# Decoder layer on one core: the first sequence's cross-attention maxima are split one tile sooner, and their transfer is issued ahead of the next queries' pieces

## The reference

```
x = x + self_attention(layernorm(x))          # 16 heads of 16, 4 key/value heads, causal, rotary
x = x + cross_attention(layernorm(x), ctx)    # 16 heads of 16, keys and values from ctx, int mask
x = x + ffn(layernorm(x))                     # relu(x w1 + b1), rounded to a 4-3 float, times rounded w2

q, k = rope(q), rope(k)                       # products with cosines and sines, and their sum
scores = q k^T * 16**-0.5, masked             # -inf above the diagonal, or -1e9 where mask == 0
out = softmax(scores) v, then an output projection and a bias
```

## Time and profile before

| | |
|---|---|
| median of three runs | 1729.31 us |
| profiled execution | 1726.77 us, of which the span from first to last instruction 1725.1 us |
| PE busy | 1617.5 us, 94% |
| PEld / DVE / ACT / POOL busy | 56% / 67% / 65% / 44% |
| granted clock of TensorE, mean | 0.982 of full speed |
| SP's DMA queue | 130.96 MB, 51.0% of 16 engines' span |
| chain that ended last | PE 75%, DMA 9% (of the span, Q<-negT 5%), ACT 6%, DVE 4% |

### The profile page before, as it was taken

How to read it: one execution, slowest core, us unless ns; L and a number is a source line. 1 busy time by engine, 2 the same in 40 slices (tenths; PEclk the granted TensorE clock), 3 DMA queues, 4 the chain that set the end, 5 groups by cost and what they waited for, 6 DMA issues and landing times.

```text
span 1725.1 us, 33722 instructions
## 1 busy us (share of the span) xinstructions
PE 1617.5 (94%) x11950; PEld 973.6 (56%) x11950; DVE 1159.0 (67%) x1736; ACT 1116.1 (65%) x1733; POOL 753.5 (44%) x1010
## 2 busy tenths in 40 slices
PE   3879999999999999999999999999999999999988
PEld 2445556656555565655656555665655556565555
DVE  4557576685857758586676858668585775857573
ACT  4455675766668566665856567576666856666574
POOL 2252344644345553444545334464434555344410
PEclk7979999999999999999999999999999999999999
DMA  7473453754547374553845546375454737454420
GB/s 182 59 99 70 68 85 65 103 95 64 96 60 107 68 96 90 75 84 57 119 72 81 94 66 89 65 103 95 64 96 60 106 68 96 90 75 73 62 40 13
DMA packets 106238, 140.17 MB, mean 81 GB/s; under 512 B 12385, under 2 KB 74242, under 8 KB 105954
## 3 DMA queue, kind: packets, MB, share of 16 engines
q1 hardware_dynamic: 103090, 130.96, 51.0%
q0 software_dynamic: 2352, 8.26, 1.5%
q10 hardware_dynamic: 768, 0.57, 0.1%
HBM read 21.29 MB, written 8.39 MB: 17 GB/s over the span
## 4 chain that ended last, share of the span: by engine, by line
PE 75%; DMA 9%; ACT 6%; DVE 4%; issue 3%; POOL 2%; SPq 1%; DVEq 0%; ACTq 0%; POOLq 0%
PE o_pair L1457 14%; PE score L1418 8%; PE small L1543 7%; DMA Q<-negT 5%; PE small L1577 5%; PE o_pair L1288 5%; PE small L1288 4%; PE score L1395 3%; PE small L1304 3%; PE score L1341 3%; DVE negmax L1021 2%; PE score L1376 2%; PE small L1470 2%; DMA sums<-o_sb 2%; PE score L1400 2%
## 5 line engine op out<-in xcount | busy, mean ns | idle before, releaser
L1021 DVE TENSOR_REDUCE negmax<-score 128x4 f32<-128x1024 f32 (+1 forms) x384 | 456.9, 1216 | 73.4 <-PE score L1376 47.0
L780 ACT ACTIVATE P<-score 128x1024 f32<-128x1024 f32 x448 | 446.4, 1026 | 74.6 <-PE score L1418 26.4
L1053 DVE TENSOR_TENSOR P<-P,cross_bound 128x1024 f32<-128x1024 f32 x192 | 230.8, 1250 | 88.6 <-ACT P L780 88.5
L1457 PE MATMUL o_pair<-P,V 128*32 128x256 f32 (+1 forms) x4096 | 280.0, 362 | 2.6 <-DVE P L1053 2.4
L828 ACT ACTIVATE score<-cross_q 128x1024 f32<-128x1024 bf16 x192 | 196.3, 1023 | 46.4 <-DVE negmax L1021 42.9
L1418 PE MATMUL score<-Q,K 99*128 99x256 bf16 x1024 | 152.3, 276 | 25.9 <-DMA Q<-negT 24.8
L1457 PEld LDWEIGHTS o_pair<-P,V 128*32 128x32 f32 x4096 | 87.8, 108 | 134.6 <-issue 73.4
L1577 PE MATMUL small<-xnT,w 128*128 128x256 f32 x600 | 157.6, 381 | 0.0
L1418 PEld LDWEIGHTS score<-Q,K 99*128 99x128 bf16 x1024 | 83.7, 98 | 125.7 <-ACT P L780 61.7
L558 POOL TENSOR_TENSOR x<-x,ffn 128x1024 f32<-128x1024 f32 x15 | 32.8, 2189 | 268.9 <-DVE negmax L1021 268.9
L1376 PE MATMUL score<-K,Q 96*128 96x256 bf16 x768 | 121.0, 282 | 9.9 <-ACT score L828 5.4
(11 more groups left out here) (202 smaller groups left out, 3049.4 us busy)
## 6 DMA issues: line engine op xcount, KB each, us to landing
K<-k2p SPq DMA_DIRECT2D x96, 256.0 KB, 6.2
Q<-q2p SPq DMA_DIRECT2D x192, 128.0 KB, 5.2
Q<-q1p SPq DMA_DIRECT2D x90, 256.0 KB, 6.7
x_in<-in_x SPq DMA_DIRECT2D x16, 512.0 KB, 5.3
ctxT<-in_ctx SPq DMA_DIRECT2D x16, 512.0 KB, 7.1
k2f<-q1f SPq DMA_DIRECT2D x32, 256.0 KB, 6.3
inT<-o_sb SPq DMA_DIRECT2D x60, 128.0 KB
o<-inverse SPq DMA_DIRECT2D x60, 128.0 KB
```

The costliest lines, as they stand in the source:

```text
L780: A.activation(P[:, t % 4, :], score[b][:, :, :], ACT.Exp, scale=SCALE).then_inc(score_free[b], 1)
L1021: V.tensor_reduce(negmax[:, k, h:h + 1024 // w], s.rearrange("p (h w) -> p h w", w=w), AX.X, ALU.max, negate=True).then_inc(score_free[b], 1)
L1053: V.tensor_tensor(p, p, cross_bound[:, t % 2, :].unsqueeze(1).broadcast_to([128, 4, SEQ]), ALU.min).then_inc(probs_masked[1], 1)
L1457: last = T.matmul(o_ps[ob][32 * j:32 * j + 32, SEQ * gg + q0:SEQ * gg + SEQ], v, p, start=s == 0, stop=end, tile_position=(0, 32 * j), ski ...
```

## The change

Three orders are changed; no instruction is added or taken away.

- On ACT, in the plain cross scores: `cut_first` of the first sequence stands ahead of tile 10's premask instead of behind it, `cut_second` behind that premask instead of behind tile 11's premask and eviction, and `maxima` behind tile 12's premask and eviction instead of behind tile 13's premask.
- On POOL: `cut_rest` stands between the products and the sum of the rotated keys, and `cut_third` behind that sum. Before, both stood behind the first query piece.
- On SP: `put_neg` of the first sequence stands ahead of the three transfers of the first query piece instead of behind them.

```diff
--- before.py
+++ after.py
@@ -458,9 +458,9 @@
                 if nxt:
                     sp.wait_ge(small_full[st.bank("v2_1")], st.this("v2_1"))
                     sp.dma_start(ctxT[:, :, :], ctx_v[i + 1]).then_inc(ctx_loaded, 16)
+                put_neg(st, 1, 0)
+                if nxt:
                     put_part("q1", 0, i + 1)
-                put_neg(st, 1, 0)
-                if nxt:
                     put_part("k1", 0, i + 1)
                     put_part("q1", 1, i + 1)
                     put_part("k1", 1, i + 1)
@@ -644,11 +644,12 @@
                     rope_products("q1", cosq, sinq, q1s, i + 1)
                     rope_sum("q1", q1s, i + 1)
                     rope_products("k1", cosk, sink, k1s, i + 1)
+                cut_rest(1, i, 0)
+                if nxt:
                     rope_sum("k1", k1s, i + 1)
+                cut_third(1, i, 0)
+                if nxt:
                     part("q1", 0, whole, part1, i + 1)
-                cut_rest(1, i, 0)
-                cut_third(1, i, 0)
-                if nxt:
                     rest("q1", i + 1)
                     part("k1", 0, whole, part1, i + 1)
                     part("q1", 1, rest1, part2, i + 1)
@@ -934,15 +935,15 @@
                 if prev:
                     hidden(st, [2])
                 for t in range(3, N2):
+                    if t == 10:
+                        cut_first(1, i, 0)
                     if t not in PE_MASKED:
                         premask(i, t)
                     if prev and t in EVICT_AFTER:
                         hidden(st, [3 + EVICT_AFTER.index(t)])
                     if t == 10:
-                        cut_first(1, i, 0)
-                    if t == 11:
                         cut_second(1, i, 0)
-                    if t == 13:
+                    if t == 12:
                         maxima(st, 1, 0)
                 if prev:
                     ffn_out(st, 0)
```

More of the change, by code:

```diff
@@ L460, in body @@
                     sp.dma_start(ctxT[:, :, :], ctx_v[i + 1]).then_inc(ctx_loaded, 16)
-                    put_part("q1", 0, i + 1)
                 put_neg(st, 1, 0)
                 if nxt:
+                    put_part("q1", 0, i + 1)
                     put_part("k1", 0, i + 1)
@@ L646, in body @@
                     rope_products("k1", cosk, sink, k1s, i + 1)
+                cut_rest(1, i, 0)
+                if nxt:
                     rope_sum("k1", k1s, i + 1)
-                    part("q1", 0, whole, part1, i + 1)
-                cut_rest(1, i, 0)
                 cut_third(1, i, 0)
                 if nxt:
+                    part("q1", 0, whole, part1, i + 1)
                     rest("q1", i + 1)
```

## The result

The changed kernel took 1780.28 us (median of six runs, 1776.22 to 1783.95) against 1728.55 for the kernel before on the same chip: ratio 1.0296, 95% interval 1.0277 to 1.0315, 51.7 us slower. The forecast was 1740, with a range up to 1754. Its profiled execution is 1777.49 us, the span 1775.9, the mean granted clock 0.961 (0.982 before).

The account below looks back on a forecast made before the run. Bound: TensorE's own stream plus its recurring wait for the first maxima. Steady pairs +7.8, first pair -3.1, second -0.7, clock +6.8: together +10.8, 1737.6 us on the profile's scale, about 1740 as median; range 1715 to 1754.

Parts of the forecast that it names:

- The wait ahead of tile 0: Shifted cross scores: TensorE's 1.64 us wait for the first maxima goes, first scores start at 745.5, 1.9 us sooner.
- The second maxima are held: Ahead of tile 8: q1's and k1's pieces delay them, 2.4 us wait, 0.6 us later per steady pair, +7.8.
- I take 757.45: SP's queue: assumed landing of the second maxima, within bounds 756.6 and 757.9; tile 8 then starts at 757.6.
- The first pairs: First two pairs: -3.1 us as the 3.3 us idle mostly goes, and -0.7 us in the second.
- The clock: Behind the tile 8 wait: falls to half speed cost 4 x 1.7 = +6.8 us.
- I take 4 of 13: Steady pairs: number assumed to have a 3.4 us stretch at half speed, 1.7 us each.
- 0 and 13 times: Steady pairs: bounds set on how often the clock falls behind the tile 8 wait.
- the rival that had 8%: Steady pairs: the clock falls in nearly every pass, 13 x 2.3 - 3.8 = +26 us, 1755 us; chance 8%.

Follow-up runs that it names:

- one_ahead: The changed kernel with one of the three first q1 pieces issued ahead of the first maxima, the other two behind; 1717.08 us, ratio 0.9918.
- k1_behind: one_ahead with k1's two second-part pieces issued behind the second maxima; 1702.46 us, ratio 0.9841.
- x_first: bulk_behind with x_in issued right behind the second maxima, ahead of q1's and k1's second parts; 1700.95 us, ratio 0.9841.
- engines_only: The changed kernel with SP's order put back, leaving ACT's and POOL's half alone; 1750.53 us, ratio 1.0120.
- bulk_behind: The changed kernel with the second parts of q1 and k1 issued behind the second maxima; 1749.60 us, ratio 1.0112.
- own_queue: The changed kernel with the second maxima issued by ACT in its own DMA queue instead of by SP; 1837.8 us, ratio 1.0640.
- tail_spread: The changed kernel with the second maxima sent as three one-row transfers of 8 KB instead of one of three rows; 1787.39 us, ratio 1.0330.
- half_filled: The changed kernel with 14 extra matmuls of 256 columns per pass ahead of TensorE's wait for the second maxima; 1763.31 us, ratio 1.0199.

## Why the prediction was wrong

The mechanism was the one forecast; two terms of the sum were too small, the landing of the second maxima and, above all, the clock.

- **The wait ahead of tile 0** goes: right. Tile 0 starts 1.8 us sooner (forecast 1.9), the maxima are issued at 740.2 on the old scale (forecast 740.1), q1 at 741.1 (forecast 740.9). ACT and POOL keep up but for one premask, for which TensorE now waits 0.40 us instead of 0.23.
- **The second maxima are held**: right in kind, shown by one_ahead, k1_behind and x_first, which change nothing but the order in SP's queue. The size was wrong. "I take 757.45, near today's last landing shifted, since today's sum already holds one such small transfer": that is the first step that failed. The first maxima did leave the sum, but among the pieces they had cost k1's last landing only 0.3 us (16.6 against 16.3 behind q1), while the second ones, behind the last piece, add 1.3 us of their own. 17.5 us measured against 16.5; tile 8 starts 1.8 us later instead of 0.6, and the pass without the clock's part is 1.6 us longer. Term: 13 x 1.6 = +20.8 instead of +7.8.
- **The first pairs**: right in the sum, in part by luck. SP's third context issue in the passes stands at 313.5 against 317.1 before, -3.6; the forecast for the first two pairs was -3.8. Its parts are others: 0.9 us later at the first issue, 4.7 gained to the second (the idle, and one stretch at 0.50 less), 0.2 lost to the third, where -3.1 and -0.7 were forecast.
- **The clock** is the second step that failed, and the larger error. Forecast were 4 single stretches for 6.8 us ("I take 4 of 13"), "as the gap is longer than today's, but most passes around it are dense". Measured were 23 stretches behind all 13 waits, 13 x 2.5 = +32.5, or 1.4 us a stretch. The bound "0 and 13 times" was itself wrong: it counted one stretch a wait, and 1.7 us each. The two rows at hand, falls after 1.65 and 2.37 us of idle, spoke for a fall in nearly every pass, the rival that had 8%; even its 1755 lacks the second stretches and the late landing.
- **The sum**: 20.8 - 3.6 + 32.5 = 49.7, of 50.8 us between the two profiled spans (51.7 between the medians). The rest lies in the last pass: the changed kernel has a stretch at 0.50 at 1747.8, behind an idle of 2.38 us that before had too, as long and in the same place (1697.3), with the clock at 1.00 behind it. From this idle to the next one it is 23.3 us against 21.6. Why the clock fell in one and not in the other is open.
- What the forecast didn't see, though it didn't decide here: POOL's cuts ahead of its first query piece delay q1 by 0.8 us where q1 is not held by the maxima (engines_only).

## What to carry to other kernels

In one in-order queue a small urgent transfer put at the head can hand its wait to the next small one behind the bulk, as here: list every transfer of the queue with its issue and its due time, and give way to both by moving what is due last (k1_behind, x_first). Look also at what stands behind what you moved (bulk_behind). And price an idle of TensorE with the clock that follows it: here the clock cost more than the later landing, 2.5 against 1.6 us a pass, though 1.6 us of idle ahead of tile 0 had cost no clock at all.

## What the runs showed of the hardware

- The transfer issued on ACT's queue did not run beside SP's 1.3 MB already queued: its first packet came over 9 us after the issue (own_queue).
- What a small transfer adds at the end of a full queue has little to do with its bytes. 64 KB pieces landed some 0.5 us apart and the 24 KB of the maxima 1.3 us behind the last of them (changed kernel); three transfers of 8 KB landed 0.3 to 0.75 us apart (tail_spread).
- The clock fell to 1.2 GHz for one to three stretches of 3.4 us at each idle of 3.3 us ahead of tile 8. Single falls followed idles of 2.4 us ahead of tile 0 in 5 of 13 steady passes (engines_only) and of 1.6 ahead of tile 8 in 11 of 13 (half_filled). None followed 1.6 us ahead of tile 0 (before), nor 1.1 ahead of tile 8 in twelve passes (one_ahead).
